# 32 of the 80 tiles of attention probabilities of a pair of heads are turned by VectorE's 32-blocks and DRAM instead of TensorE

## What is computed

```python
k = jnp.einsum('ihd,bpd->biph', W_K, x)          # q and v alike
scores = jnp.einsum('biph,biqh->biqp', k, q)
masked = scores * mask - jnp.float32(10000000000.0) * (1.0 - mask)
attn = jax.nn.softmax(masked / jnp.sqrt(jnp.float32(d_head)), axis=-1)
z = jnp.einsum('biqp,biph->biqh', attn, v)
...
x = _layernorm(x + attention(x), axis=-1)
x = _layernorm(x + experts(x), axis=-1)
```

## Time and profile before

| | before |
|---|---|
| median of 3 runs | 2503.51 us |
| the profiled execution's own time | 2492.34 us |
| its span, first to last instruction | 2490.6 us |
| busy in the span: PE, DVE, ACT, POOL | 97%, 71%, 58%, 14% |
| attention | from the start to about 1600 us |
| mean granted clock of TensorE | 0.990 |

### The profile page before, as it was taken

How to read it: one execution, slowest core, us unless ns; L and a number is a source line. 1 busy time by engine, 2 the same in 40 slices (tenths; PEclk the granted TensorE clock), 3 DMA queues, 4 the chain that set the end, 5 groups by cost and what they waited for, 6 DMA issues and landing times. The chain is left out here.

```text
span 2490.6 us, 40355 instructions
## 1 busy us (share of the span) xinstructions
PE 2413.5 (97%) x13946; PEld 2110.3 (85%) x13946; DVE 1759.6 (71%) x3651; ACT 1436.1 (58%) x3216; POOL 345.0 (14%) x366
## 2 busy tenths in 40 slices
PE   7999999999999999999999999899999999999993
PEld 6888888888888888888888888688899989999993
DVE  5775766667567667667577576678748888888885
ACT  4554555456456456456455455555437777777774
POOL 0000000000000000000000000167631121122211
PEclk9999999999999999999999999999999999999997
DMA  7321421421430421322322133278649999999997
GB/s 261 114 67 56 139 64 58 139 65 28 136 97 24 130 95 41 126 69 67 100 94 67 60 120 111 82 276 314 223 138 305 307 312 304 313 310 312 301 311 208
DMA packets 193179, 394.88 MB, mean 159 GB/s; under 512 B 23689, under 2 KB 73225, under 8 KB 182992
## 3 DMA queue, kind: packets, MB, share of 16 engines
q1 hardware_dynamic: 165520, 332.79, 39.5%
q0 software_dynamic: 27456, 59.51, 10.3%
HBM read 294.35 MB, written 106.48 MB: 161 GB/s over the span
## 5 line engine op out<-in xcount | busy, mean ns | idle before, releaser
L519 ACT ACTIVATE pT_hi<-turned 128x512 fp32r<-128x512 f32 (+3 forms) x640 | 334.1, 535 | 239.9 <-PE turned L781 239.0
L508 ACT ACTIVATE probs<-bank,neg_max 128x512 f32<-128x512 f32 (+3 forms) x640 | 396.8, 626 | 129.2 <-DVE neg_max L623 96.2
L630 DVE TENSOR_TENSOR pT_lo<-turned,pT_hi 128x512 fp32r<-128x512 f32 (+3 forms) x640 | 373.9, 602 | 60.2 <-ACT pT_hi L519 59.9
L617 DVE TENSOR_REDUCE max_part<-bank 128x1 f32<-128x512 f32 (+2 forms) x576 | 353.5, 621 | 80.6 <-PE bank L767 68.7
L781 PE MATMUL turned<-ident,probs 128*128 128x128 f32 x2176 | 328.9, 273 | 0.1
L754 PE MATMUL bank<-x_sb,w_hi 128*128 128x512 f32 x992 | 312.1, 396 | 11.6 <-DVE x_sb L583 11.6
L781 PEld LDWEIGHTS turned<-ident,probs 128*128 128x128 f32 x2176 | 264.2, 140 | 49.3 <-PE bank L741 0.3
L796 PE MATMUL z_ps<-pT_hi,v_hi 128*128 128x512 f32 (+3 forms) x640 | 258.8, 404 | 7.6 <-DVE pT_lo L630 5.2
L767 PE MATMUL bank<-k_hi,q_hi 128*128 128x512 f32 (+2 forms) x640 | 253.2, 396 | 0.4 <-DVE k_lo L596 0.2
L1919 DVE TENSOR_TENSOR up_lo<-w_raw,up_hi 128x704 fp32r<-128x704 f32 x256 | 217.0, 886 | 37.0 <-ACT up_hi L1406 36.4
L767 PE MATMUL bank<-k_hi,q_lo 128*128 128x512 f32 (+2 forms) x640 | 234.0, 366 | 0.0
(11 more groups left out here) (213 smaller groups left out, 5153.0 us busy)
## 6 DMA issues: line engine op xcount, KB each, us to landing
w_raw<-in_w SPq DMA_DIRECT2D x256, 352.0 KB, 5.4
x_sb<-x_parts SPq DMA_DIRECT2D x60, 1024.0 KB, 6.1
w_raw<-in_w SPq DMA_DIRECT2D x128, 256.0 KB, 5.7
rows_in<-gathered_x SPq DMA_DIRECT2D x64, 263.5 KB, 5.3
spread_sb<-inv_dram POOLq DMA_DIRECT2D x64, 256.0 KB, 3.5
z_dram<-z_sb SPq DMA_DIRECT2D x64, 256.0 KB, 2.4
z_raw<-z_dram SPq DMA_DIRECT2D x16, 1024.0 KB, 5.3
w_raw<-in_w_qkv SPq DMA_DIRECT2D x32, 384.0 KB, 8.8
```

Of the source, the lines that this page charges most:

```text
L508: nc.scalar.activation(probs[:, u % 2, r, kc * CHUNK:kc * CHUNK + used], bank[:, job_at["s", h, c, r, kc] % BANKS, 0:used], ACT.Exp, bias= ...
L519: nc.scalar.activation(pT_sb[0][:, n % TURNS, lo_col:], turned[:, n % TURNS, lo_col:], ACT.Copy).then_inc(turn_hi, 1)
L617: nc.vector.reduce_max(max_part[:, row % ROWS, kc:kc + 1], bank[:, job % BANKS, 0:used], axis=AX_X).then_inc(part_done, 1)
L630: nc.vector.tensor_tensor(pT_sb[1][:, n % TURNS, lo_col:], turned[:, n % TURNS, lo_col:], pT_sb[0][:, n % TURNS, lo_col:].bitcast(F32), AL ...
```

## The change

It does these things, all in the attention:

1. **Far tiles.** `FAR` names 2, 5 and 9 tiles of each head in chunks 1, 2 and 3: 32 of the 80 tiles of a pair, all of full width, 128 of its 272 blocks of 128 x 128. They are no longer transposed by TensorE. In a new step `blocks` VectorE turns all 32 x 32 blocks of the 128 x 512 tile, reading every fourth column of `probs`, into one of two slots of `stage` (L718); SP stores the slot to one of 4 slots of `far_dram` (L504); POOL reads it back with its rows rearranged, in pieces of 128 numbers, to the place in `probs` where it was (L434). The copy to `pT_hi` and the subtraction for `pT_lo` then read `probs` instead of `turned`.
2. **Order of rows.** So that both kinds of tiles agree, the 512 rows of a chunk now stand as 4 quads of 32 columns of each row tile. The near transposes write four runs of 32, the diagonal `pv` reads and writes 4 runs, and `result` puts the rows back.
3. **x** is loaded from ScalarE's queue (L610), right behind its copy of the last v of a chunk.
4. **Empty rows and weights** are issued by SP one at a time: behind each unit's store of `z_sb` two stores of empty rows, and behind the first three one load of `w_raw`.
5. `spread_sb` and `z_sb` have one buffer instead of two.
6. **Waits.** `blocks` waits for the exponentials of its tile and for the store two far tiles back; an `exp` that overwrites `probs` waits for the subtraction of far tiles there.
7. **ORDER** is a new table, of 476 steps for 444.

```diff
+FAR = {1: range(2, 4), 2: range(3, 8), 3: range(3, 12)}
...
+        "b": [("blocks", 0, *tile) for tile in tiles if tile[2] in FAR.get(tile[1], ())],
...
-        spread_sb = sb("spread_sb", [P, 2, CHUNK], F32)
-        z_sb = sb("z_sb", [P, 2, CHUNK], F32)
+        spread_sb = sb("spread_sb", [P, CHUNK], F32)
+        z_sb = sb("z_sb", [P, CHUNK], F32)
+        stage = sb("stage", [P, 2, CHUNK], F32)
...
+            def fetch(i, h, c, j):
+                m = far_at[h, c, j]
+                slot = m % FAR_SLOTS
+                wait_apart(pool, waited, far_out[m % 2], far_count(i, m, 2))
+                pool.dma_start(far_place(h, c, j), far_dram[slot].rearrange("(a j) (b m) -> (j b) a m", a=QUADS, b=QUADS)
+                               ).then_inc(far_in[slot], 16)
...
+                    if step[0] == "blocks":
+                        m = far_at[step[2:]]
+                        slot = m % FAR_SLOTS
+                        sp.wait_ge(blocks_made, i * n_far + m + 1)
+                        if i or m >= FAR_SLOTS:
+
+                            sp.wait_ge(far_in[slot], far_count(i, m - FAR_SLOTS, FAR_SLOTS))
+                        sp.dma_start(far_dram[slot], stage[:, m % 2]).then_inc(far_out[m % 2], 16)
...
+                        empty = gathered_x[i * (EXPERTS // PAIRS) + u]
+                        sp.dma_start(empty[:, 0:EMPTY], empty_row[:, 0:EMPTY]).then_inc(zero_out, 16)
+                        sp.dma_start(empty[:, EMPTY:], empty_row[:]).then_inc(zero_out, 16)
+                        if u < W_SLOTS and not last:
+                            sp.wait_ge(w_split, upto(i, DT, -1))
+                            load_w(i + 1, u)
...
+            def load_x(c):
+
+                act.wait_ge(x_stored[0], x_stored_all[0])
+                for n in range(2):
+                    act.wait_ge(x_stored[c], x_stored_all[c])
+                    act.dma_start(x_sb[:, n].bitcast(F32), x_parts[c, n].rearrange("p (t n) -> p t n", t=DT)).then_inc(x_in, 16)
...
+            def blocks(i, h, c, j):
+
+
+                m = far_at[h, c, j]
+                dve.wait_ge(exp_done, upto(i, n_exp, exp_at[h, c, RPC - 1, j // RPC]))
+                if i or m >= 2:
+
+                    dve.wait_ge(far_out[m % 2], far_count(i, m - 2, 2))
+                nc.vector.transpose(stage[:, m % 2].rearrange("p (b r n) -> p r b n", b=QUADS, r=RPC),
+                                    probs[:, unit_at[h, c] % 2, :, j * P:(j + 1) * P].rearrange(
+                                        "p r (n b) -> p r b n", b=QUADS)).then_inc(blocks_made, 1)
...
             def turn(i, h, c, j):
+                if (h, c, j) in far_at:
+                    return
```

More of the change, by code:

```diff
@@ L208, in attention @@
     turn_at, pv_at, unit_at = counted("turn"), counted("pv"), counted("out")
+    far_at = counted("blocks")
+    near_at = {tile: n for n, tile in enumerate(tile for tile in turn_at if tile not in far_at)}
+    n_far, n_near = len(far_at), len(near_at)
+    FAR_SLOTS = 4
+    BLOCK = 32
+    QUADS = P // BLOCK
+    assert n_far % FAR_SLOTS == 0
     assert counted("inverse") == unit_at
@@ L259, in attention @@
         x_raw_in = [sem(f"x_raw_in{c}") for c in range(CHUNKS)]
-        x_first_in = [sem(f"x_first_in{dt}") for dt in range(DT)]
+        x_first_in = x_raw_in[:1] + [sem(f"x_first_in{dt}") for dt in range(1, DT)]
         x_hi = sem("x_hi")
@@ L282, in attention @@
         inv_free = sem("inv_free")
-        spread_in = [sem(f"spread_in{n}") for n in range(2)]
+        spread_in = sem("spread_in")
         waited = sem("waited1")
+        blocks_made = sem("blocks_made")
+        far_out = [sem(f"far_out{n}") for n in range(2)]
+        far_in = [sem(f"far_in{n}") for n in range(FAR_SLOTS)]
         z_done = sem("z_done")
@@ L326, in attention, with by_quad, far_count, far_place @@
         pieces_after_job = {job: x_pieces[DT + n * per_job:DT + (n + 1) * per_job] for n, job in enumerate(early)}
+        def by_quad(ap, first=0):
+            return ap.rearrange("p (a m) -> p a m", a=QUADS)[:, :, first * BLOCK:]
+        def far_count(i, m, slots):
+            return 16 * (i * n_far // slots + m // slots + 1)
+        def far_place(h, c, j):
+            return probs[:, unit_at[h, c] % 2, :, j * P:(j + 1) * P]
+        def turned_tile(h, c, j):
+            if (h, c, j) in far_at:
+                return far_place(h, c, j)
+            return by_quad(turned[:, turn_at[h, c, j] % TURNS], max(0, j - RPC * c))
+        def turned_parts(part, h, c, j):
+            return by_quad(pT_sb[part][:, turn_at[h, c, j] % TURNS], max(0, j - RPC * c))
+        def last_of(at, h, c, j):
+            before = [tile for tile in at if turn_at[tile] <= turn_at[h, c, j]]
+            return at[max(before, key=lambda tile: turn_at[tile])] if before else -1
+        def wait_turned(eng, i, h, c, j):
+            if last_of(near_at, h, c, j) >= 0:
+                eng.wait_ge(turn_ready, upto(i, n_near, last_of(near_at, h, c, j)))
+            far = [tile for tile in far_at if turn_at[tile] <= turn_at[h, c, j]]
+            last_far = max((turn_at[tile] for tile in far), default=-1)
+            if last_far < 0:
+                last_far = max(turn_at[tile] for tile in far_at) - n_turns
+            if upto(i, n_turns, last_far) > 0:
+                eng.wait_ge(turn_lo, upto(i, n_turns, last_far))
         def proj_dst(part, job):
@@ L369, in spread @@
                 wait_apart(pool, inv_free, inv_stored[u % 2], i * per + 16 * (u // 2 + 1))
-                wait_apart(pool, waited, z_done, upto(i, n_units, u - 2))
-                pool.dma_start(spread_sb[:, u % 2], inv_dram[u % 2:u % 2 + 1].to_broadcast([P, CHUNK])
-                               ).then_inc(spread_in[u % 2], 16)
+            def spread(i, u):
+                wait_apart(pool, waited, z_done, upto(i, n_units, u - 1))
+                pool.dma_start(spread_sb[:], inv_dram[u % 2:u % 2 + 1].to_broadcast([P, CHUNK])
+                               ).then_inc(spread_in, 16)
+            def fetch(i, h, c, j):
[4 more added lines that the diff above has]
+                               ).then_inc(far_in[slot], 16)
             def body(i):
+                passed = []
                 for step in plan:
                     if step[0] == "inverse":
-                        spread(i, *step[2:])
+                        store_inverse(i, *step[2:])
+                    if step[0] in ("inverse", "out"):
+                        passed.append((step[0], unit_at[step[2:]]))
+                        for u in range(n_units):
+                            if passed[-1] in (("inverse", u), ("out", u - 1)) and ("inverse", u) in passed and (
+                                    u == 0 or ("out", u - 1) in passed):
+                                spread(i, u)
+                    if step[0] == "blocks":
+                        fetch(i, *step[2:])
             for i in range(PAIRS):
@@ L425, in body @@
                         sp.wait_ge(job_ready, upto(i, n_jobs, job_at["job", "v", c, 1]))
-                        if not (last and c == CHUNKS - 1):
-                            load_x((c + 1) % CHUNKS)
-                        else:
+                        if last and c == CHUNKS - 1:
                             for g in range(HEADS // GROUP):
@@ L542, in body @@
                         project(i, step[2:])
+                        if step[2] == "v" and step[4] == 1 and not (last and step[3] == CHUNKS - 1):
+                            load_x((step[3] + 1) % CHUNKS)
                     if step[0] == "exp":
```

77 lines of the change are left out of this document (34 added, 43 removed).

## The result

The changed kernel takes 2613.1 us (median of 4 runs, 2601.9 to 2618.15), the kernel before on the same chip 2502.62: a ratio of 1.045, 95% interval 1.0427 to 1.0474. It is slower by 4.5%, 110 us, where 27 us less were forecast. Nearly all of the time is lost in the attention: in the profiles the last `z_sb` is made at 1713.7 us (before, 1596.2), 117.5 us later, where the spans differ by 122.2. The profiled execution has a span of 2612.8 us and a mean granted clock of 0.971 (before, 0.990).

What follows compares the result with a forecast made beforehand. TensorE was taken to bound the kernel. Seven pairs gain 14.5 - 8.4 - 2.0 = 4.1 us each, the last loses 1.5: 27 us less, from 2503.5 to 2476 us; forecast 2455 to 2495 (chance 0.47), whole range 2435 to 2520.

Steps and rivals of the forecast that it cites:

- What bounds the kernel: In the attention TensorE's own instructions set the pace; removing 128 transposes a pair saves 14.5 us a pair.
- The block at z's price, 1.08 us: VectorE's block transpose costs as much as z, which also reads with a stride: 1.08 us, 1.00 start to start.
- my two ends: Bounds for the block transpose: 0.57 us with stride and turning free, 1.48 with z's surcharge once more for the turning.
- rivals 1 and 2: Block transposes cheap, below 0.8 us: 2435 us, chance 0.17; or dear, 1.48 us: 2509 us, chance 0.10.
- VectorE the longer by 8.4 us in chunk 3: In head 0's chunk 3 stretch VectorE has 39.8 us of work, TensorE 31.4, so TensorE waits 8.4 a pair.
- ORDER, x, single buffers, empties at nothing: Loading x on ScalarE's queue, single buffers, empty rows and weights cost nothing; the new order got no price of its own.
- The round trip is hidden: A far tile's block, store and fetch take 8.2 us, covered by VectorE's work before the copy: no cost.
- Rival 3: Slow fetches make the trip 13.0 us, delaying ScalarE before exponentials: 42 us slower, 2518 us; chance 0.15.
- rival 5: TensorE's clock falls in the waits, once a pair at 1.7 us: 13 us in all, 2489 us; chance 0.07.
- Waits elsewhere than in chunk 3's scores: Sign of a wrong forecast: TensorE's idle time, some 10 us a pair, lying elsewhere, as in chunks 1 and 2.

Runs made afterwards that it cites:

- e14: The change with 24 far tiles, only the first key chunk's maximum taken, and an order made for both: 2421.6 us.
- e17: e14 without its far tiles, in the same order with the block letters taken out: 2494.2 us.
- e16: The change with block transposes reading 32 neighbouring columns instead of every fourth, so the output differs: 2544.3 us.
- e1: The change without any far tile, its new order and all other edits kept: 2576.9 us.
- e2: The change with its block transposes, but without the far tiles' store and fetch and the waits for them: 2521.0 us.
- e5: The kernel before with only its ORDER replaced by the new one, block letters taken out: 2615.4 us.
- e6: e1 with the ORDER of the kernel before: 2504.1 us.
- e4: The change with SP storing from probs instead of stage, so block transposes no longer wait for the store two far tiles back: 2555.1 us.
- e13: e1 with 14 letters of its order moved by at most ten places each: 2533.4 us.
- e12: The kernel before with only the first key chunk's maximum taken: 2484.1 us.

## Why the prediction was wrong, point by point

- *What bounds the kernel*: right. TensorE's 14.5 us a pair came off as counted; with room for them, 9.1 of 10.8 us came through (e14, e17).
- *The block at z's price, 1.08 us*: right, 1.087. Of my two ends, free stride and a second surcharge, neither holds: the stride is 0.39, the turning 0.699 - 0.566 = 0.13, if the cheapest neighbour is the measure. So my rivals 1 and 2 are both out. The Trainium skill (SBUF - State Buffer, the note on SBUF cachelines) has a penalty for each access that crosses to a new line. e16 agrees in direction: 0.39 us for 512 such accesses in place of 128, less than the 0.53 that I reckoned for a full halving.
- *VectorE the longer by 8.4 us in chunk 3*: the count of VectorE's work was right, what it does to TensorE only in part. The stretch that I had counted runs in the trace from 578.7 to 621.1 us, 42.4 us for my 39.8, with VectorE busy for 40.5 and TensorE for 35.8. Of TensorE's 6.6 idle us 2.6 are waits for `pT_lo`, as forecast, and 3.8 are waits for banks that exponentials still read. In e1, without any block, the same stretch of the list has 4.4 us of that second kind. Over the whole kernel blocks without the trip cost 60 us in the new order (e2, by the estimate above), where the sum had 7 x 10.4 + 16.0 = 89.
- *ORDER, x, single buffers, empties at nothing*: this is the step that failed. I counted in the new list only VectorE's work against TensorE's over one long stretch. I did not count what TensorE has between a row's last score and the next use of its banks, a matter of 2 to 3 us in which no sum of busy times tells anything. The old list keeps this so well filled that its view of waits, 300 to 1500 us, has none for an exponential's bank at all; the new one without far tiles has 72 in 1200 us (e1). In place of nothing the order cost 112 us in e5 and 73 beside the other edits (e1). For x, the buffers, the empties and the quads "nothing" was right in the old order (e6); in the new one they are worth 38 us (e5 against e1). Of the 137 us between forecast and measurement this term is 73. The other 64 are the far tiles, which were to give 27 us and cost 36.
- *The round trip is hidden*: wrong. Store and fetch land after 3.5 and 4.0 us, where I took 2.4 and 3.5. The copy waits 36.8 us in 1200 for its fetch, once 7.5 us. The larger part I had not seen: a block waits for the store two far tiles back, in VectorE's queue, with the maxima and subtractions behind it, 65.6 us in 1200; without it 58 us come back (e4). This is the second step that failed. Rival 3 had its sign, and with 42 us some size of it, but by another path: a late fetch on ScalarE. That its number is near is luck.
- *The clock*, rival 5: real and priced too low. I gave one fall of 1.7 us a pair. In the pair looked at it fell twice, to 0.86 and 0.80 at 520 to 530 us and to 0.89 and 0.77 at 605 to 615, and the attention's mean is 0.97: about 5.5 us a pair. Not every gap does it: at 595 to 600 us TensorE was idle for 2.1 of 5 us, and the clock read 1.00 there and in the next 5.
- *Waits elsewhere than in chunk 3's scores*, the sign that I had named for "wrong", is what the profile showed: chunk 1 (520 to 525 us, 2.8 idle) and the rows of chunk 2 and 3. So is the wait of ScalarE for the fetch, for which I had named 2 us as the limit: 7.5. A pair takes 207 us instead of 192, with TensorE idle for 18 instead of 10.

Still open: the 26 us above the kernel before that e13's 14 letters left. TensorE is idle there for 15.5 us in 1200 (before, 3.0), about 2 us a pair or 17 in all; its weight loads wait 22.9 us in 1200 for banks and 7.2 for `z_sb`. I have not shown that these are the whole rest. Open too is what 46 of the far tiles' 152 us are made of, beyond the wait for `stage`.

## What to carry to other kernels

In a kernel with an order written out by hand, a new order is an edit with a price of its own: run it without the thing it was made for, and the old one with all else that is new, before you judge either. Where a ring of buffers fills with each unit of work, count in the list what the bounding engine has between the last write of a unit and the next use of its first buffer, and set it against the whole chain through the other queues, copies in front of it included. Work moved to an engine with 30% to spare on the average is paid wherever that engine is full for longer than the bounding one can run ahead (here 60 of 116 us, e2), and a transfer that holds one of two staging slots blocks all that is queued behind the wait.

## What the runs showed of the hardware that I had not expected

- A block transpose of 128 x 512 float32, SBUF to SBUF: 1.087 us reading every fourth column, 0.699 at unit stride.
- A 2 KB store landed after 7.6 us with x and six stores of empty rows in flight (e5), after 5.3 in the same place of e1, with x alone beside it, and after 1.7 at quiet places of both.
- Behind a window of 5 us in which TensorE was idle for half of the time, its granted clock was 0.70 and 0.61 in the next two windows, between its levels of 1.2 and 2.4 GHz, and 1.00 behind them (e5, 525 to 545 us). Behind a window in which it was idle for 2.0 of 5 us it stayed 1.00 (e1, 515 to 525).
- A TensorE that is busy for 299.0 of 300 us had still 18 us in all to gain (e12): its busy time does not show the waits of the weight loads, 13.1 us in 1200, which have a row of their own.
- Transposes into runs of 32 columns in PSUM last as long as into one run of 128: a mean of 273 ns in e6, 272 before.
